# Row maxima of the adjacency in four pieces of 1024 columns instead of two of 2048

## The reference

```python
# layer 0: graph attention
h = relu(layernorm(x))
scores = (h @ W @ a1)[:, None] + (V @ W @ a2)[None, :]
e = where(scores > 0, scores, 0.2 * scores)
attention = softmax(where(adj > 0, e, -9e15), axis=1)
x = x + elu(attention @ V + h)
# layer 1: sum over neighbours
h = relu(layernorm(x))
agg = einsum('ji,jd->id', adj, h)          # adj transposed times h
x = x + relu(agg @ U.T / adj.sum(axis=0)[:, None])
```

## Time and profile before

| | |
|---|---|
| median of 3 runs | 499.16 us (498.29 to 499.17) |
| profiled execution | 499.07 us, span 497.1 us |
| TensorE matmul busy | 433.2 us, 87% |
| VectorE busy | 299.9 us, 60% |
| ScalarE busy | 250.3 us, 50% |
| GpSimd busy | 96.2 us, 19% |
| guards (L657) | 66 of 125 x 2048, 153.3 us |

### The profile page before, as it was taken

How to read it: one execution, slowest core, us unless ns; L and a number is a source line. 1 busy time by engine, 2 the same in 40 slices (tenths; PEclk the granted TensorE clock), 3 DMA queues, 4 the chain that set the end, 5 groups by cost and what they waited for, 6 DMA issues and landing times.

```text
span 497.1 us, 8564 instructions
## 1 busy us (share of the span) xinstructions
PE 433.2 (87%) x3672; PEld 199.2 (40%) x3672; DVE 299.9 (60%) x411; ACT 250.3 (50%) x289; POOL 96.2 (19%) x85
## 2 busy tenths in 40 slices
PE   0414778889998999998999989999999999999996
PEld 0311323444333444333454333354333336645563
DVE  3539999678999469999649999623443313101011
ACT  1211222266776776766877667766777741100010
POOL 0440360511131402233401223100110001200000
PEclk9975855599999999999999999999999999999999
DMA  9699999999999880000000000000000000000001
GB/s 164 73 109 107 107 105 107 106 107 109 101 102 101 88 90 9 1 1 1 1 1 1 1 1 1 2 1 1 1 1 1 1 1 1 1 12 10 22 15 30
DMA packets 17837, 21.11 MB, mean 42 GB/s; under 512 B 13412, under 2 KB 13476, under 8 KB 17799
## 3 DMA queue, kind: packets, MB, share of 16 engines
q0 software_dynamic: 4752, 16.90, 32.9%
q1 hardware_dynamic: 8606, 2.18, 2.2%
q10 hardware_dynamic: 4441, 1.49, 1.9%
HBM read 69.79 MB, written 1.05 MB: 143 GB/s over the span
## 4 chain that ended last, share of the span: by engine, by line
PE 62%; DVE 17%; issue 10%; ACT 4%; DMA 4%; ACTq 2%; POOL 1%; DVEq 0%; POOLq 0%
PE att L953 18%; PE q L934 10%; PE den L956 10%; DVE junk L657 10%; PE q L1035 7%; DVE arena L703 4%; DMA adj_sb<-in_adj_dram 4%; PE q L1005 3%; PE den L1035 3%; PE att L1035 2%; PE z L898 2%; PE z L912 2%; ACT q L493 2%; ACT arena L477 2%; ACTq L379 1%
## 5 line engine op out<-in xcount | busy, mean ns | idle before, releaser
L657 DVE CUSTOM_DVE_ANT_0 junk<-adj_sb,t_row 125x2048 uint8<-125x2048 uint8 x66 | 153.3, 2323 | 8.6 <-DMA adj_sb<-in_adj_dram 8.5
L703 DVE SCALAR_TENSOR_TENSOR arena<-arena,b_col,q 128x1000 f32<-128x1000 f32 (+1 forms) x96 | 90.6, 949 | 85.4 <-PE q L934 85.4
L953 PE MATMUL att<-arena,v_sb 128*64 128x500 f32 x512 | 136.2, 610 | 3.6 <-DVE scratch L711 1.6
L481 ACT ACTIVATE arena<-arena,t 128x1000 f32<-128x1000 f32 (+1 forms) x96 | 84.4, 884 | 106.9 <-DVE arena L703 106.7
L934 PE MATMUL q<-bi,adj_sb 128*128 128x125 bf16 x1056 | 89.6, 222 | 18.7 <-DVE arena L703 9.2
L934 PEld LDWEIGHTS q<-bi,adj_sb 128*128 128x128 fp8e4 x1056 | 62.9, 99 | 78.8 <-issue 43.6
L956 PE MATMUL den<-arena,ones 128*32 128x250 f32 x1024 | 81.0, 388 | 0.0
L493 ACT ACTIVATE q<-arena,minus_b 128x1000 f32<-128x1000 f32 x64 | 70.1, 1096 | 4.9 <-ACT arena L477 0.7
L477 ACT ACTIVATE arena<-q,t_col 128x1000 f32<-128x1000 f32 x64 | 69.0, 1078 | 1.7 <-PE q L934 1.6
L956 PEld LDWEIGHTS den<-arena,ones 128*32 128x32 f32 x1024 | 20.2, 108 | 102.0 <-issue 102.0
L329 POOL TENSOR_TENSOR buf_a<-buf_a,g_sb 125x512 f32<-125x512 f32 (+1 forms) x5 | 11.2, 2230 | 128.4 <-DVE buf_a L735 111.5
(11 more groups left out here) (153 smaller groups left out, 315.7 us busy)
## 6 DMA issues: line engine op xcount, KB each, us to landing
adj_sb<-in_adj_dram POOLq DMA_DIRECT2D x33, 500.0 KB, 45.9
v_sb<-n_L_gnn_entity_embs_dram ACTq DMA_DIRECT2D x4, 256.0 KB, 9.1
x_sb<-in_x_dram SPq DMA_DIRECT2D x1, 928.0 KB
out_dram<-x_sb SPq DMA_DIRECT2D x7, 124.0 KB
adj_sb<-junk ACTq DMA_DIRECT2D x1, 396.0 KB
x_sb<-in_x_dram SPq DMA_DIRECT2D x1, 125.0 KB
out_dram<-x_sb SPq DMA_DIRECT2D x1, 125.0 KB
buf_a<-in_L_gnn_a_dram ACTq DMA_DIRECT2D x1, 32.0 KB, 2.9
```

The lines of the kernel that those rows point to most:

```text
L481: nc.scalar.activation(e_part(n % E_SLOTS, nb), e_part(n % E_SLOTS, nb), ACT.Exp, bias=t02[:, c:c + 1])\
L657: nc.vector.tensor_tensor_reduce(out=junk[0:R, :], in0=adj_bytes[0:R, b, half], in1=t_row[0:R, half], scale=1.0 / ONE, scalar=0.0, op0=ALU ...
L703: nc.vector.scalar_tensor_tensor(out=e_part(n % E_SLOTS, nb), in0=a_part(nb), scalar=b_col[:, c:c + 1], in1=part(q[0 if nb > 1 else n % Q_ ...
L953: nc.tensor.matmul(att[h * D:(h + 1) * D, 0:4 * R], v_sb[:, c, :], e[:, h * 4 * R:(h + 1) * 4 * R], start=first, stop=final)
```

## The change

Each row maximum is taken in four pieces of 1024 columns. A block now has four guards, so a group of eight has 32, which `guards_at` spreads over tiles 0 to 25. `row_shifts` joins four numbers a row with two maxima instead of one. `scratch` is cut from 1000 to 752 columns (its users take at most 750), and `g_max` grows.

```diff
+    PIECES = 4
+    PIECE = M // PIECES
...
-        scratch = sb("scratch", [P, 1000])
+        scratch = sb("scratch", [P, 752])
...
-        g_max = sb("g_max", [P, 2, NB])
+        g_max = sb("g_max", [P, PIECES, NB])
...
-            pieces = [(b, h) for b in range(first, last) for h in range(2)]
+            pieces = [(b, h) for b in range(first, last) for h in range(PIECES)]
             n = len(pieces)
             return [pieces[k] for k in range(n) if k * 26 // n == c]
...
-                half = slice(h * HALF, (h + 1) * HALF)
+                half = slice(h * PIECE, (h + 1) * PIECE)
...
-                order = b * 2 + h
+                order = b * PIECES + h
                 if order >= 1:
                     dve.wait_ge(guarded, order)
-                nc.vector.tensor_tensor_reduce(out=junk[0:R, :], in0=adj_bytes[0:R, b, half], in1=t_row[0:R, half], scale=1.0 / ONE,
+                nc.vector.tensor_tensor_reduce(out=junk[0:R, 0:PIECE], in0=adj_bytes[0:R, b, half], in1=t_row[0:R, half], scale=1.0 / ONE,
...
-                dve.wait_ge(guarded, 2 * b1)
+                dve.wait_ge(guarded, PIECES * b1)
+                pairs = g_max[0:R, 0:2, b0:b1]
+                nc.vector.tensor_tensor(pairs, pairs, g_max[0:R, 2:4, b0:b1], ALU.max).then_inc(guard_paired, 1)
+                dve.wait_ge(guard_paired, i + 1)
                 nc.vector.tensor_tensor(top, top, g_max[0:R, 1, b0:b1], ALU.max).then_inc(guard_joined, 1)
...
-            guard(0, 0)
-            guard(0, 1)
+            for h in range(PIECES):
+                guard(0, h)
```

More of the change, by code:

```diff
@@ L160, in graph_layers_kernel @@
                                                          sem("guard_joined"))
+        guard_paired = sem("guard_paired")
         shifts_turned, bi_made, a_made, a_copied = sem("shifts_turned"), sem("bi_made"), sem("a_made"), sem("a_copied")
```

## The result

The changed kernel is slower: 503.75 us median of 4 runs (502.71 to 503.91) beside 498.73 us for the kernel before, ratio 1.0098 with a 95% interval of [1.0077, 1.0119]. Run again beside 15 runs of the kernel before it gave 503.04 us for 499.07, ratio 1.0082 [1.0055, 1.0109]. Its profiled execution has 503.86 us and a span of 501.9 us, 4.8 us more than before.

What follows compares the result with a forecast made beforehand. VectorE's sum of work was taken to set the pace in groups 0, 2 and 3, with group 1 near balance. Terms 1.3 + 0.2 + 1.3 + 0.7 = +3.5 us on 499.07 gave 502.6 us, range 499.9 to 505.5.

Steps and rivals of the forecast that it cites:

- What bounds the kernel: Whole kernel: VectorE's sum of work counts in groups 0, 2 and 3, and group 1 is near the balance.
- The price of a piece: VectorE's guards: a quarter costs 1.14 us start to start, 1.26 ahead of another guard, 1.27 ahead of the join.
- the upper bound of 1.41 us a piece: Quarter's price if its fixed part were a whole narrow VectorE instruction, 0.34 us; said to give about +19 us.
- Group 0, +1.3: Up to 103 us: block 0 +0.4, join +0.19, pieces to `scores` of tile 24 +0.7, last quarter covered by TensorE.
- Group 1, +0.2: Group 1: +0.2 ahead of tile 0, then +1.1 with 1.1 filled by waits; between -0.5 and +1.3.
- Group 2, +1.3: Group 2: pieces +2.2 us, less 0.8 of waits and some 0.1 where VectorE waits for GpSimd.
- from there to tile 24: Group 2, from `copy_den` to tile 24: quarters take 33.2 us where halves took 31.1, +2.2.
- Group 3, +0.7: Group 3 up to tile 22: pieces +2.0 us, less 1.2 of waits and 0.1.
- Smoothing wins: Rival, groups 1 to 3: smaller largest loads between `scores` gain 0.8 us each, group 1 2.0 more; 496.0 us, chance 0.11.
- The piece costs its whole duration: Rival, all guards: next instruction starts only when a guard ends, 1.22 us a quarter; +7.7, 506.8 us, chance 0.09.
- TensorE's clock comes back later: Rival: the 9.00 us at clock 0.71 lengthen, or slowed guards beside GpSimd multiply; 1 to 2 us more, 504.3, chance 0.08.
- No difference: Rival: extra work partly hidden, ScalarE's queue being later in groups 2 and 3; about 499.4 us, chance 0.10.

Runs made afterwards that it cites:

- early halves: Kernel before the change, with the first two, three and three guards of groups 2, 3 and 4 run one group earlier: 492.18 us, ratio 0.9877.
- eighths: Changed kernel with eight pieces of 512 columns a row and one more maximum in the join: 529.5 us, ratio 1.0623.
- the experiment that fills that wait: Changed kernel with `copy_den` of groups 2 to 4 behind the guard of tile 2 instead of ahead of it: 503.71 us, ratio 1.0123.
- the old places: Changed kernel with both quarters of a half standing where that half stood before the change: 510.4 us, ratio 1.0261.
- two buffers: Changed kernel with two buffers for the guards' unused output, so a guard waits for the guard two ahead: 499.29 us, ratio 1.0024.

## Why the prediction was right

The direction and the mechanism were right, the size was 1.3 us short: 499.07 + 3.5 was forecast for the profiled execution and it took 503.86, +4.8. By its own steps:

- *What bounds the kernel.* Right. Removing VectorE's work from the stretch gives 6 us (early halves), adding it costs 31 (eighths), and in each the stages answer one by one.
- *The price of a piece.* Right to 0.01 us: 1.15 and 1.26 for 1.14 and 1.26; mean duration 1252 ns, with some long ones, as forecast. The forecast didn't know of what the 0.12 us between guards consists; it is the wait for the semaphore. By its own counts (118 quarters) the upper bound of 1.41 us a piece gives about +30 us and not +19; nothing in the forecast hangs on that.
- *Group 0, +1.3.* It was +2.25, and +2.3 already at the first turn. The last quarter is covered, as said: the chain leaves VectorE at 92.22, and that quarter starts at 93.79. Block 0 (+0.40), the join (+0.19) and the pieces came as computed. Missing were 0.38 us in which VectorE stood for no reason that the profile shows (42.97; the other seven profiles of kernels with quarters in group 0 have 0.37 to 0.39 us there, those with eighths or halves none, so it comes with the code, but its cause stays open), 0.33 us of longer guards beside GpSimd, and 0.12 us by which the first guard starts later.
- *Group 1, +0.2.* It was 0.0, with the low clock in both profiles; at the full clock, halves in this group take 74.04 us and quarters 74.01. The wait at tile 4 grew to 1.66 us, 1.7 forecast.
- *Group 2, +1.3.* It was +1.1, close by luck in part, since the reason was partly another. The step "from there to tile 24" named `copy_den` as the start of the solid stretch, and the experiment that fills that wait shows it false: TensorE sets tile 4. From tile 4 on the sum is 15 x 1.15 + 9 x 1.26 - 12 x 2.21 = +2.1, less 0.57 and 0.38 us of filled waits, plus 0.18 of long guards, +1.3, for 49.07 - 47.96 = +1.1 measured.
- *Group 3, +0.7.* This term was mis-sized: +1.5. From tile 4 to 22 the pieces give 14 x 1.15 + 8 x 1.26 - 11 x 2.21 = +1.9 and filled waits -1.35; long quarters give +1.1, which the sum had at nothing (the clock's rival named slowed guards, but with a price taken from nowhere in this stage). GpSimd's operations cut short bring this group to 76.25 us, 0.2 below the kernel before.
- *Smoothing wins.* Fell for this kernel: with the old places it is worse, but the evener ones don't make up for the prices. Its reason isn't empty: with two buffers group 1 gained 1.1 us against the kernel before.
- *The piece costs its whole duration.* Fell: duration 1.22, start to start 1.15. The Trainium skill's "VectorE: DVE Perf Modes", section "The DRAIN you can't avoid", names the rule that this rival took, but adds that a next operation which isn't held starts earlier; the 1.15 us agree with the addition and not with the rule alone.
- *TensorE's clock comes back later.* Not seen: from the first turn to the call of `rows` it took 5.17 us for 5.24 before. The other half of this rival, slowed guards beside GpSimd's work, did come, on top of the forecast: +0.33, +0.18 and +1.13 us in groups 0, 2 and 3.
- *No difference.* Fell: groups 2 and 3, where it put ScalarE's queue last, lost 1.1 and 1.5 us.

## What to carry to other kernels

An engine with 60% busy time can be the bound of half a kernel: take start-to-start times of its instructions between two fixed points and compare the sum with the pace of the engine that looks like the bound. Where that sum is over, cutting its work finer costs the fixed part of each piece, and a piece that waits for its neighbour's semaphore pays more for that wait than for being cut. Before evening out such work, look for the places where the engine waits anyway and move whole pieces there.

## What the runs showed of the hardware

- A guard's wait for the guard directly ahead costs 0.11 us although both are on VectorE: 1.26 us start to start with it, 1.15 us when it waits for the one two ahead.
- A VectorE instruction with two SBUF operands and a GpSimd operation wait for each other's end (GpSimd's ends 0.98 us after the guard, the next guard 1.08 us after GpSimd's). With VectorE in `scores` behind a guard GpSimd's turn is free; between two guards it cost 0.71 to 0.97 us each in groups 2 and 3.
- TensorE's granted clock from 110 to 113 us, and in the counting matmuls, differs from profile to profile (0.53 or 1.00; 0.66, 0.83 or 1.00), in steps worth 1.5 to 1.6 us. These profiles are of different kernels; that one kernel alone has such steps is seen in the mean clock of the kernel before, 0.932 to 0.943 over its executions, and in the two profiles of the changed kernel, where the turns of group 0 took 5.17 and 4.62 us to the call of `rows`. What decides it stays open.
